# A row-wise state-space scan on one core: own sums moved into the spreading weights, TensorE's products put in order of their shape, statistics every four rows, y normalised by ScalarE

## The reference

```python
dA_cs = jnp.cumsum(dt * A, axis=2)
Lmat = jnp.exp(dA_cs[:, :, :, None, :] - dA_cs[:, :, None, :, :])
att = where(causal, einsum('bcihn,bcjhn->bcijh', Ch, Bh) * Lmat * dt, 0)
y_intra = einsum('bcijh,bcjhp->bcihp', att, x)
states = einsum('bcjhn,bcjh,bcjhp->bchpn', Bh, exp(last - dA_cs) * dt, x)
state = state * exp(last) + states            # from chunk to chunk
y_inter = einsum('bcihn,bcih,bchpn->bcihp', Ch, exp(dA_cs), state_before)
y = y_intra + y_inter + D * x
y = (y - mu) / sqrt(var + eps) * norm_w + norm_b
out = (y * z) @ out_proj_w.T                  # z: gate, in_proj of the pixel
```

## Time and profile before

| what | value |
|---|---|
| time, median of three runs | 2428.84 us (2423.58 to 2432.23) |
| the profiled execution's own time | 2429.54 us |
| its span | 2427.7 us |
| granted TensorE clock, mean | 0.958 of full speed |
| busy share of the span | PE 87%, DVE 68%, ACT 54%, POOL 46% |
| the scan's loop | 837 to 1816 us |

### The profile page before, as it was taken

How to read it: one execution, slowest core, us unless ns; L and a number is a source line. 1 busy time by engine, 2 the same in 40 slices (tenths; PEclk the granted TensorE clock), 3 DMA queues, 4 the chain that set the end, 5 groups by cost and what they waited for, 6 DMA issues and landing times. The chain is left out here.

```text
span 2427.7 us, 64964 instructions
## 1 busy us (share of the span) xinstructions
PE 2108.2 (87%) x23257; PEld 1587.5 (65%) x23384; DVE 1643.5 (68%) x3164; ACT 1301.4 (54%) x2727; POOL 1109.9 (46%) x1392
## 2 busy tenths in 40 slices
PE   0596997999899399999999999999987969879798
PEld 0473645888788277777777777777765646356463
DVE  5345585765565578888888888888874555735557
ACT  0254540085058567777777777777743545335453
POOL 0333250000000277777777887878763332533325
PEclk9998997999999699999999999999998989989899
DMA  9624595415723422222222222222216145961459
GB/s 218 184 82 74 117 331 150 127 26 194 222 31 127 146 52 62 59 58 58 58 58 58 58 58 58 58 58 59 60 45 185 35 88 150 308 183 42 88 139 320
DMA packets 305632, 272.30 MB, mean 112 GB/s; under 512 B 175966, under 2 KB 238846, under 8 KB 299210
## 3 DMA queue, kind: packets, MB, share of 16 engines
q1 hardware_dynamic: 294698, 256.00, 38.1%
q0 software_dynamic: 9280, 6.44, 2.4%
q10 hardware_dynamic: 1496, 7.63, 1.0%
HBM read 165.29 MB, written 81.46 MB: 102 GB/s over the span
## 5 line engine op out<-in xcount | busy, mean ns | idle before, releaser
L1701 DVE TENSOR_TENSOR l_scan_att<-l_scan_decay,l_scan_causal_scores 128x512 f32<-128x512 f32 x384 | 319.3, 832 | 64.4 <-ACT l_scan_decay L1670 64.1
L722 ACT COPY l_arena<-l_body_bank 128x384 f32<-128x384 f32 x192 | 142.0, 901 | 262.8 <-PE l_body_bank L590 262.8
L1664 ACT ACTIVATE l_scan_decay<-l_scan_cum 128x512 f32<-128x512 f32 x384 | 216.2, 597 | 33.1 <-PE l_scan_cum L1556 33.0
L1670 ACT ACTIVATE l_scan_decay<-l_scan_decay 128x512 f32<-128x512 f32 x384 | 227.8, 630 | 4.1
L1681 ACT ACTIVATE l_scan_yw<-l_scan_y_by_channel,l_scan_norm_b,l_scan_norm_w 128x128 f32<-128x128 f32 x384 | 148.0, 455 | 125.4 <-PE l_scan_y_by_channel L1618 118.4
L1603 PE MATMUL l_scan_gate_projected<-l_scan_xr,l_wf 97*128 97x128 f32 (+1 forms) x1536 | 205.3, 283 | 1.3 <-DVE l_scan_xo L1756 1.2
L652 PE MATMUL l_body_bank<-l_arena 100*64 100x128 f32 x2304 | 150.0, 286 | 59.8 <-DMA l_arena<-l_arena 59.8
L570 POOL TENSOR_TENSOR l_arena<-l_arena 96x512 f32<-96x512 f32 x96 | 122.7, 1278 | 168.8 <-ACT l_arena L788 162.8
L1521 POOL TENSOR_TENSOR l_scan_inter<-l_scan_inter,l_scan_xd 128x384 f32<-128x384 f32 x128 | 128.1, 1000 | 156.7 <-DVE l_scan_inter L1716 156.7
L1634 PE MATMUL l_scan_gate_projected<-l_scan_yz,l_scan_wo 128*96 128x128 f32 x1536 | 198.5, 279 | 1.1 <-DVE l_scan_yz L1733 1.1
L1634 PEld LDWEIGHTS l_scan_gate_projected<-l_scan_yz,l_scan_wo 128*96 128x96 f32 x1536 | 171.0, 163 | 40.0 <-issue 33.9
(11 more groups left out here) (191 smaller groups left out, 4814.9 us busy)
## 6 DMA issues: line engine op xcount, KB each, us to landing
l_scan_xc<-convolved_rows SPq DMA_DIRECT2D x128, 224.0 KB, 2.8
x_after<-l_arena SPq DMA_DIRECT2D x64, 384.0 KB, 4.9
l_arena<-x_after SPq DMA_DIRECT2D x64, 384.0 KB, 5.6
convolved_rows<-l_slots SPq DMA_DIRECT2D x48, 441.0 KB
l_conv_x_main<-x_after SPq DMA_DIRECT2D x64, 256.0 KB, 3.0
l_arena<-x_after SPq DMA_DIRECT2D x16, 1024.0 KB, 8.6
prepare_xt<-x SPq DMA_DIRECT2D x8, 1536.0 KB, 9.4
l_arena<-x SPq DMA_DIRECT2D x32, 384.0 KB, 5.5
```

Source lines behind the costliest of these rows:

```text
L722: nc.scalar.copy(tA[:, b, :, j:j + 2].rearrange("p c q -> p q c"), bank[n % 4][:, 0:2 * C].rearrange("p (q c) -> p q c", q=2)).then_inc(t_ ...
L1664: nc.scalar.activation(decay[:, b % 2, 4 * g:4 * g + 4, :], cum[(b + g) % 2][:], ACT.Relu, scale=-1.0)\
L1670: nc.scalar.activation(group, group, ACT.Exp, scale=-1.0).then_inc(exp_done, 1)
L1701: nc.vector.tensor_tensor(att[:, b, 4 * g:4 * g + 4, :], decay[:, b % 2, 4 * g:4 * g + 4, :], causal[:, b % 2:b % 2 + 1, :].broadcast_to([ ...
```

## The change

In words: the own sum of a pixel no longer comes from a wide product. The tile `lift` takes the place of `pick` and `unpick`: for each of four slots the ones of `pick`, and in three more partitions the row's own sums, copied there by SyncE with three small DMAs in each turn (12 partitions of 128 bf16 values into one partition). The padding of `cum_t` is -1 in place of 0, so the same four products per group subtract them. TensorE's order is regrouped by shape. The chunk's state goes to its own half of the bank (`half_s`) and is made ahead of the product with the state. ScalarE makes yn from y, rstd and a shift of -mean * rstd, which VectorE makes in a [128, 1] operation. VectorE's order of the new state, attention 1, sum with x and attention 2 changes, and it takes statistics once in four rows over 512 columns. SyncE issues x of the gate and the store a turn later, and starts its loads only when all constants stand.

```diff
-                nc.gpsimd.memset(parts[:], 0.0).then_inc(padded, 1)
+                nc.gpsimd.memset(parts[:], -1.0).then_inc(padded, 1)
@@ SyncE
+                sp.wait_ge(ready, CONST)
...
+                        if not (isinstance(r, int) and r < U):
+                            hold(sp, cum_done, 3 * (r - 3), passed)
+                        for part in range(3):
+                            own = 64 * (b % 2) + 3 * N_HEADS + part
+                            first = 64 * (b % 2) + part * N_HEADS
+                            sp.dma_start(lift[own:own + 1, b], cum_t[first:first + N_HEADS, bass.ds(n * 2 + b // 2, 1), :])                                .then_inc(lift_landed[b], 16)
-                    if row := at(1):
+                    if row := at(2):
...
-                    row = at(1)
+                    row = at(2)
@@ TensorE, cumulative
-                    nc.tensor.matmul(bank[:].rearrange("p h w -> p (h w)"), pair, unpick[:, heads, :].rearrange("p h w -> p (h w)"),
-                                     start=True, stop=False)
+                    if g == 0:
+                        pe.wait_ge(lift_landed[b], n * 48 + 48)
                     for h in range(4):
-                        last = nc.tensor.matmul(bank[:, h, :], pick[:, (b % 2) * N_HEADS + 4 * g + h, :], pair,
-                                                start=False, stop=(h == 3))
+                        last = nc.tensor.matmul(bank[:, h, :], lift[:, b, 4 * g + h, :], pair, start=(h == 0), stop=(h == 3))
@@ TensorE, turn
+                    if row0:
+                        cumulative(row0, 0)
...
+                        nc.tensor.transpose(p_bcg[:, 0, :], xc[:, b, CONV_DIM + N_STATE - 128:], ident[:]).then_inc(bc_turned, 1)
                     if row2:
...
+                        for g in range(2):
+                            last = nc.tensor.matmul(p_i[g * N_STATE:(g + 1) * N_STATE, 0, half_s], xc[:, b, D_INNER:D_INNER + N_STATE],
+                                                    xw[:, b % 2, g * D_INNER // 2:(g + 1) * D_INNER // 2], start=True, stop=True)
+                        last.then_inc(st_done, 1)
...
                     if row0:
-                        cumulative(row0, 0)
-                        cumulative(row0, 1)
...
+                        cumulative(row0, 1)
...
-                    if row2:
-                        r, b, n = row2
-                        pe.wait_ge(scaled, r + 1)
...
@@ ScalarE, turn: gaps(0), B and C, yt, decays(0), yn, gaps(1), decays(1), yw, gaps(2), decays(2)
+                    if row3:
+                        r, b, n = row3
+                        act.wait_ge(turned, r)
+                        act.wait_ge(shift_done, r + 1)
+                        nc.scalar.activation(yn[:, b % 2], y[:, b % 2], ACT.Identity, bias=shift[:, b], scale=rstd[:, b]).then_inc(yn_done, 1)
@@ VectorE
-                nc.vector.tensor_copy(pick[:], spread(spreads[:], 128)).then_inc(ready, 1)
-                nc.vector.tensor_scalar(unpick[:], spread(spreads[:], 128), -1.0, None, ALU.mult).then_inc(ready, 1)
+                for b in range(U):
+                    heads = slice((b % 2) * N_HEADS, (b % 2 + 1) * N_HEADS)
+                    nc.vector.tensor_copy(lift[:, b], spread(spreads[:, heads], 128)).then_inc(ready, 1)
...
-                        dve.wait_ge(turned, r)
                         dve.wait_ge(rstd_done, 2 * r + 2)
-                        nc.vector.tensor_scalar(yn[:, b % 2], y[:, b % 2], mv[:, b, 0:1], rstd[:, b], ALU.subtract, ALU.mult)\
-                            .then_inc(yn_done, 1)
+                        nc.vector.scalar_tensor_tensor(out=shift[:, b], in0=mv[:, b, 0:1], scalar=-1.0, in1=rstd[:, b], op0=ALU.mult, op1=ALU.mult)\
+                            .then_inc(shift_done, 1)
...
+                        if not (isinstance(r, int) and r < 2):
+                            dve.wait_ge(yn_done, r - 1)
                         dve.wait_ge(y_back, r + 1)
...
-                        for kk in range(2):
-                            nc.vector.bn_stats(stats[:, kk, bass.ds(r, 1), :], xo[:, b, kk, :]).then_inc(stats_done, 1)
+                        if b == U - 1:
+                            for kk in range(2):
+                                nc.vector.bn_stats(stats[:, kk, bass.ds(n, 1), :], xo[:, kk].rearrange("p u w -> p (u w)")).then_inc(stats_done, 1)
```

More of the change, by code:

```diff
@@ L1386, in scan_rows @@
         half = ph.sb("minus_half", [128, 1])
-        pick = ph.sb("pick", [128, 2 * N_HEADS, 128], BF16)
-        unpick = ph.sb("unpick", [128, 2 * N_HEADS, 128], BF16)
+        lift = ph.sb("lift", [128, U, N_HEADS, 128], BF16)
         xc = ph.sb("xc", [128, U, CONV_DIM + N_STATE])
@@ L1406, in scan_rows @@
         rstd = ph.sb("rstd", [128, U, 1])
+        shift = ph.sb("minus_mean_rstd", [128, U, 1])
         yw = ph.sb("yw", [128, 2, 3, W])
         yz = ph.sb("yz", [128, 3, W])
-        xo = ph.sb("xo", [CH, U, 2, W])
+        xo = ph.sb("xo", [CH, 2, U, W])
         cum = [ph.ps(f"cum{j}", [128, 4, W]) for j in range(2)]
@@ L1621, in turn @@
                         cumulative(row0, 2)
-                    if row2:
-                        r, b, n = row2
-                        pe.wait_ge(scaled, r + 1)
-                        for g in range(2):
-                            last = nc.tensor.matmul(p_i[g * N_STATE:(g + 1) * N_STATE, 0, half_i], xc[:, b, D_INNER:D_INNER + N_STATE],
-                                                    xw[:, b % 2, g * D_INNER // 2:(g + 1) * D_INNER // 2], start=True, stop=True)
-                        last.then_inc(st_done, 1)
                     if row4:
@@ L1646, in turn, with gaps, decays @@
                     row0, row2, row3 = (at(lag) for lag in (0, 2, 3))
+                    def gaps(g):
+                        r, b, n = row0
+                        act.wait_ge(cum_done, 3 * r + g + 1)
+                        nc.scalar.activation(decay[:, b % 2, 4 * g:4 * g + 4, :], cum[(b + g) % 2][:], ACT.Relu, scale=-1.0)\
+                            .then_inc(gap_done, 1)
+                    def decays(g):
+                        r, b, n = row0
+                        act.wait_ge(gap_done, 2 + 3 * r + g + 1)
+                        group = decay[:, b % 2, 4 * g:4 * g + 4, :]
+                        nc.scalar.activation(group, group, ACT.Exp, scale=-1.0).then_inc(exp_done, 1)
+                    if row0:
+                        r, b, n = row0
+                        act.wait_ge(att_done, 3 * r)
+                        gaps(0)
+                        act.wait_ge(bc_turned, r + 1)
+                        if not (isinstance(r, int) and r < U):
+                            act.wait_ge(inter_done, r - 2)
+                        nc.scalar.copy(bct[0:N_STATE, b, 0, :], p_bcg[N_STATE:2 * N_STATE, 0, :])
+                        nc.scalar.copy(bct[:, b, 1, :], p_bcg[2 * N_STATE:4 * N_STATE, 0, :]).then_inc(bc_copied, 1)
                     if row2:
@@ L1683, in turn @@
                     if row0:
-                        r, b, n = row0
                         gaps(2)
```

54 lines of the change are left out of this document (19 added, 35 removed).

## The result

| | before | after |
|---|---|---|
| median of four runs each, us | 2426.21 (2423.51 to 2432.23) | 2339.91 (2336.92 to 2343.44) |
| ratio, with its 95% interval | | 0.9634 (0.9606 to 0.9662) |
| profiled execution, us | 2429.54, span 2427.7 | 2336.92, span 2335.1 |
| mean turn from the ninth on, us | 7.535 | 6.726 |
| start of the scan to the ninth transpose of B and C, us | 59.7 | 65.6 |

The change makes the kernel 3.7% faster; 2325 was forecast, with 2280 to 2400 as the range. The last two lines are from the starts of the transpose (L1580 before, L1575 after). The profiled times differ by 92.6 us. Of these, 119 turns x (7.535 - 6.726) = 96.2 are the steady turns. The first turns give back 6.0. The scan starts 2.2 us later, and what stands behind its last transpose takes 4.6 us less; both lie in phases that vary by a few us between executions.

The account below looks back on a forecast made before the run. TensorE alone was taken to set the 7.535 us turn; afterwards loops through GpSimd would, at 6.65. 123 turns x (7.535 - 6.65) = 109 us off, 4 on: 2429 to 2325 us, range 2280 to 2400.

Parts of the forecast that it names:

- TensorE's turn: TensorE's own work per scan turn, without wide products and with fewer shape changes: 6.05 to 6.4 us, taken as 6.25.
- The rival in which the gaps belong to the waits: TensorE's gaps come from each wait, not from shape changes; order brings nothing, turn 6.9 us, time 2355; chance 0.08.
- The sum: Ordinary turn 6.5 us plus 0.1 to 0.2 for every fourth turn's statistics: 6.65 us a turn, 2325 us in all.
- Second loop: VectorE and GpSimd: scaling, skip addition, products, two rstd steps, shift, handoffs: 6.0 us, or 6.4 with the power held up.
- First loop: GpSimd's products into TensorE's L1573, chunk state and L1586, then VectorE's scaling, GpSimd's skip addition and products, handoffs: 6.5 us.
- The sign given beforehand: In the changed profile TensorE would wait for GpSimd before L1573's successor, or for yz before the output projection.
- The port: Shared by VectorE and GpSimd: two stalls a turn, 0.46 and 0.42 us; small operations don't hold it long; load 6.0 us.
- the rival of the whole port: VectorE and GpSimd lock the port for whole instructions: 7.1 us a turn, with waits 6.9 to 7.4, 2355 to 2416; chance 0.20.
- The pair at 1304.7: GpSimd's power (0.57 us) and VectorE's attention product (0.69 us) ran side by side, neither longer: evidence against a whole-instruction lock.
- Cost nothing: SyncE's seven issues a turn, 0.43 us each, some 3.7 in all, fit in 4.9 us of waiting for xo.
- my slower rival: Copies of own sums in SyncE's queue: seven issues set the turn above 7.5 us; at 1.2 us each 2540 us; chance 0.05.
- Start: At the scan's start SyncE's loads wait for VectorE's four constant copies; row 0 is ready at 841.1, 3.7 us lost.

Follow-up runs that it names:

- xo last: The changed kernel with VectorE's sum with x (xo) put behind the third attention product (attention 2): 2347.62 us, ratio 0.9674 to the kernel before.
- shift late: The changed kernel with VectorE's shift computed behind the scaling instead of ahead of it: 2336.47 us, ratio 0.9612 to the kernel before.

## Why the prediction was right, point by point

**TensorE's turn**: forecast 6.05 to 6.4, taken 6.25. Measured 6.77 fully busy with the wide products; less their 0.65 that is 6.12. Right; five changes of shape were saved, so 128 x 96 counts as 128 x 128. The three that are left cost 0.12, 0.30 and 0.12 us. The rival in which the gaps belong to the waits had the order bring nothing; it brought 0.77. The Trainium skill, TensorEngine Tiling (Array Packing), Key Properties, says that changing the tiling mode drains the engine. The trace agrees in so far as loads of a new shape start 0.10 to 0.30 us late with nobody to wait for; that it is a drain it doesn't show.

**The sum**, 6.65 us a turn against 6.726. The ordinary turn was to be 6.5 and is 6.57; the fourth was to add 0.1 to 0.2 and adds 0.63 / 4 = 0.16. Of the 15 us between 2325 and 2340, 9 are the turns; the rest is 2 us in the first turns and differences of a few us between executions.

**Second loop**: named, at 6.4 with the power held up. The term that was too small is the stall of the power: 0.42 on average of both cases before, but 1.194 - 0.57 = 0.62 in every turn now, because in the new turn attention 2 always meets it. That is the 0.2 that is missing.

**First loop** (GpSimd's products into L1586, 6.5): right, and it binds at 6.57, together with the second. Its terms in the turn from 1312.16: scaling 0.56 (forecast 0.55), skip addition and products 3.82 (3.86), L1586 0.68, chunk state with its change of shape 0.46 (0.69 and 0.49), L1596 to its result 0.59 (0.59). The handoffs, to GpSimd 0.17, from there to TensorE 0.21 and back to VectorE 0.08, are 0.46 in place of 0.3; this is the term that was too small. The sign given beforehand, TensorE waiting for GpSimd, came as well, in 0.26 us of idle time that the view calls "issue". What was not foreseen is that the two loops would be equally long: opening the power's brought 0.04 us (xo last) or nothing (shift late), because the products' stayed.

**The path through yz**, 0.14 us shorter, was not foreseen.

**The port.** Forecast: two stalls, small operations don't hold it for long; the rival of the whole port had 7.1. The turn decides for the forecast, but half of its reason is wrong: the power is held by 0.62 us each time, the normalisation on VectorE by 0.34, a product by 1.62. The pair at 1304.7, on which I built, is the exception, 13 turns of 53. The Trainium skill, SBUF — State Buffer, section "SBUF: two separate sides", has an exclusive lock that goes for a whole instruction to whichever of the two starts first. The sizes agree with a lock: the power stood still for 0.62 us beside an attention product of 0.68, the product for 1.62 us beside three operations that ran from 1150.89 to 1152.50. The order does not agree: by the profile power and product had begun 0.1 and 0.15 us ahead of VectorE, and it was they that were held. The profile's spans on GpSimd are rough, so no run here settles who came first. What the rival had wrong is its sum, which put all the port's work and waits in one line.

**ScalarE**: 90.36 per cent of 6.726 is 6.1 us against 5.9; the normalisation takes 0.70 us where 0.48 was put down after the copy of the same shape, which reads PSUM where the normalisation reads SBUF. **VectorE**: shift 0.153 (0.15 forecast), statistics 0.673 (0.684).

**The normalisation's move** was priced as 0.33 us of VectorE's work. It is worth 0.56 a turn, 70 us in all, since on VectorE it stood on the power's path and met GpSimd.

**SyncE**: "Cost nothing" is right, the reason too small. The copies take 0.74 to 0.82 us each and not 0.43, seven issues 5.5 us and not 3.7, and SyncE's wait for xo falls from 4.9 us a turn to 1.2:

```profile
SPq L82 <- DVE l_scan_xo L1763: 70.7, 60, 1.8
```

It costs nothing because the load of x and the store were put a turn later. I had noted that as free room; it is worth 74.5 us (2414.4 against 2339.9). The place of my slower rival, the copies in SyncE's queue, was the right one, its point not: it had them set the turn when seven issues exceed it. They do so much earlier, through a loop over two turns.

**Start**: first sums 9.9 us after the start of the scan against 6.0 to the first transpose before: the forecast 3.7 and a little. But the turns behind them lose 2 us more, where nothing was forecast; the wait for GpSimd and the lower clock in the windows above are the likely reason; no run undid them by themselves, so this is not shown. **Behind the scan**: the fold brings nothing, as forecast. VectorE's first operation of the next phase (L806) starts 47.0 us behind the scan's last transpose of B and C, against 46.0 before, and VectorE stands idle for 10.3 us ahead of it in place of 4.5.

**Part by part.** Undone one at a time, the own sums are worth 14 us (2353.9), the normalisation 70 (2409.8), SyncE's later turn 75 (2414.4), the statistics -9 (2330.8). These don't add up to the 86 of the result, nor should they: where a part is missing, the loop that it had opened sets the turn, and hides the others.

**What stays open**: whether SyncE's later turn is needed with one copy (an estimate: 1.8 us less of 14.7 over two turns is 6.45 a turn, below the 6.73 that others set); how far the turn would fall with the products' path opened too (with the power's opened as well, the path through yz would stop it at 6.57 - 0.14 = 6.43, an estimate from the rows above), for example with the chunk's state behind the state product again, and how to do it without a new meeting at the port; why the port once lets power and attention product run side by side and mostly not; the value of the new order by itself with TensorE's products unchanged in number and the other parts undone. None was tried.

## What to carry to other kernels

When the one busy engine is relieved, list every loop that passes through two turns as well as those within one, DMA queues included, and expect several to end within a tenth of a microsecond: then removing a visible wait brings nothing. Not every wait is visible, either: before calling idle time a cost of the engine's own, look whether it ends at a fixed distance behind some other engine's result, and how long it is where that result comes early. A part that looks free, as a transfer issued a turn later, may be what carries the others, so undo each part alone before crediting the sum. And before moving an operation of VectorE look at which of GpSimd's it will meet, and how long a row of its own it will join.

## What the runs showed of the hardware

- A product of GpSimd with 0.83 us of work lasted 2.45 us beside three operations of VectorE in a row (0.67, 0.41, 0.67), though one of these has an operand in PSUM: it ran for 0.15 us ahead of them and 0.69 behind, which is all of its work. The same way the power of one column grows from 0.57 to 1.20 us beside one attention product in the changed kernel, and to 1.12 in 40 of 53 turns of the one before.
- A weight load of TensorE that needs a product of GpSimd starts 0.21 us behind the product's end, whether the wait is 0.1 us or 3. Loads of a new shape start 0.10 to 0.30 us late by themselves: 1.31 us in the eight changes of a turn before, 0.54 in three.
- Issuing a copy from SBUF into one partition takes 0.74 to 0.82 us of SyncE, into three partitions 0.81, the loads and stores over many partitions 0.35 to 0.41.
- A wait of 2.86 us of a TensorE that was otherwise nearly always busy was followed by a granted clock of 0.50 for two windows of 4 us and part of a third, in which everything else of the loop waits too. One long wait in a turn cost some 6 us.
- ScalarE's scale and bias with operands by partition, 128 x 384, took 701 ns from SBUF against 478 for the plain copy from PSUM.
